# Attention with experts on one core: how the rough scores that set the softmax shift are made

## The chip, the cores and the metric

The kernel runs on one core of a Trainium2 chip. The metric is the device time of one execution in microseconds (us), lower is better. All times below are us unless marked ns.

## The reference, cut to what matters

Input x is 8 sequences of 512 tokens by 128 values, layer-normed. Then attention with 32 query heads and 16 key/value heads of width 64, a linear position bias and a causal mask; beside it a mixture of 8 experts, of which 2 serve each token; the two results are multiplied.

```python
scores = jnp.einsum('bhqd,bhkd->bhqk', q, k) / math.sqrt(HEAD_DIM)
scores = scores + bias[None]
scores = jnp.where(causal[None, None], scores, -jnp.inf)
attn = jax.nn.softmax(scores, axis=-1)
out = jnp.einsum('bhqk,bhkd->bhqd', attn, v)
...
s = _L0_attn_ref(xn, L0_attn_W_qkv, L0_attn_W_out)
g = _silu(_L0_ffn_ref(xn, ...))
x = x + s * g
```

## The kernel before, in words

The attention is cut into 64 bodies: one body is one sequence and one pair of key/value heads. A body has two slots (`sl`, one key/value head each), and a slot has two query heads (`h`), so a body makes four 512x512 causal score matrices. Bodies 0 to 31 run first, then the experts' blocks, at whose end the preparation of body 32 is mixed in, then bodies 32 to 63.

Numbers are held as two fp16 halves (hi and lo). A query head is stacked by DMA into `q_st` as 128 rows (64 of hi, 64 of lo) beside a second plane, whose rows 0 to 63 are hi again and whose row 64 holds one shift per query, in the row for the position bias; keys are stacked in `k_st` (two buffers, `par`, by the parity of the body). The softmax needs a shift per query near the row maximum. It is found from rough scores:

- M, `rough` (PE, L948 to L966): hi half of the queries times hi half of the keys, 64 rows each, the two heads of a slot as two products on the two halves of TensorE's rows, into the two banks `M_ps[0]` and `M_ps[1]`. Three rounds per slot (`ROUNDS`): query tiles 3; 0 and 2; 1. Six rounds in a body, 16 products of 128, 256, 384 or 512 columns.
- B, `peaks` (DVE, L1588): mask and minimum along each row of each of these products, one column of `spread` each; 12 tasks in a body.
- C, `turn_shifts` (PE, L968 to L977): four products of 128x128 with the identity turn `spread`, so that each head's shifts stand in one row (0, 32, 64, 96). `shifts` (ACT, L1284) copies each of the four rows, 1x512, into row 64 of the second plane of `q_st`.
- S (PE) makes the true scores of the causal part, transposed: ten groups in a body, alternating between two banks `S_ps`. E (ACT, L1295) takes the exponential of a group, L (POOL, L824) its low half, P (PE, L1025 to L1029) multiplies it with the values: 120 products in a body.
- N, A (DVE, ACT, SP) normalise and turn the result, O (PE) projects it. Q, K, V (PE) make the queries of a slot, the keys and the values; ACT then takes the hi half, DVE the lo half, SP issues the stacking DMAs (four for one slot's queries, two for one slot's keys).

What each engine does, and in which order, is a written list, `ORDER`, one table for each half: `("M0", 2, 87)` says that in window w the engine does task M0 of body w + 2; only the sequence counts, the third number merely places it. Each engine goes through its list strictly in order and waits on semaphores in front of each task, so a task that waits holds up all behind it on its engine. `G_USERS` says which of Q, K, V, O and C take turns in the two remaining PSUM banks. Before the change C of body w + 1 stands near the end of window w, and both slots' copies on ACT behind it; S0 of the next window waits for the first slot's copies (`crow0`). There is one buffer `q_st` per slot and head, so SP may stack the queries of body n only when the scores of body n - 1 are done; `q_hi` on ACT waits until the rough products have read `q_raw`.

Of the kernel before, what the change touches and what calls it, by code (L numbers as in the profile page):

```python
# [8 lines left out]
F16 = mybir.dt.float16  # L9
# [24 lines left out]
ROUNDS = [[(3, 0)], [(0, 0), (2, 128)], [(1, 0)]]  # L34
# [24 lines left out]
        [("V0", 1), ("Q0", 2), ("C0", 1)],  # L59
# [3 lines left out]
        [("V0", 1), ("Q0", 2), ("C0", 1)],  # L63
# [14 lines left out]
        ],  # L78
        "ACT": [
# [3 lines left out]
        ],  # L83
        "DVE": [
# [22 lines left out]
        ],  # L107
        "ACT": [
# [3 lines left out]
        ],  # L112
        "DVE": [
# [25 lines left out]
def build(nc, x, w_qkv, w_out, gate_w, gate_b, w1, b1, w2, b2, out):  # L139
    slopes = [float(s) for s in alibi_slopes()]  # L140
    ctx = ExitStack()
    with ctx:
# [1597 lines left out]
```

## Time and profile before

| | |
|---|---|
| median of 3 runs | 1191.23 (1187.22 to 1195.37) |
| profiled execution, its own time | 1190.88 |
| its span | 1189.1 |
| busy PE, DVE, ACT, POOL | 94%, 83%, 78%, 75% |
| rough products, L965, busy | 138.1 |
| `peaks`, L1588, busy | 451.7 |
| row copies, L1284, busy | 147.2 |

PE is TensorE's products, PEld its weight loads (they run beside products), DVE VectorE, ACT ScalarE, POOL GpSimd, SP the engine that issues most DMAs. A line such as `128*128 128x512` names a product with a 128-row, 128-column stationary operand and 512 moving columns. Successive products overlap, so the time a product holds TensorE is read from the starts of successive rows, not from its duration.

### The profile page before, as it was taken

The page shows a single profiled execution, that of the slowest core. Times are in us where ns is not written, and L with a number is a line of the kernel's source. Part 1 is how long each engine was busy: PE and PEld are TensorE (multiplying, and loading weights), DVE is VectorE, ACT ScalarE, POOL GpSimd, SP SyncE. Part 2 cuts the span into 40 slices and gives each one's busy share as a digit, 9 for nine tenths or more (in the row PEclk, how much of TensorE's full clock was granted, in tenths as well). Part 3 has the DMA queues.
Part 4 walks back from the last instruction along what each step waited for, and adds up shares of the span by engine and source line. Part 5 has one row for each costly group of instructions (what it writes and reads, how often), then busy time and mean ns, then how long its engine had stood idle before and what let it go on. Part 6 is the DMA issues. An engine that isn't in the chain of part 4 may idle for free.

```text
span 1189.1 us, 48527 instructions
## 1 busy us (share of the span) xinstructions
PE 1119.4 (94%) x16970; PEld 830.8 (70%) x16970; DVE 982.1 (83%) x3099; ACT 931.9 (78%) x1835; POOL 886.9 (75%) x1067
## 2 busy tenths in 40 slices
PE   2669999999999999998999989999999999999996
PEld 1447777777777777777888757777777777777775
DVE  7778888888888888886777878888888888888883
ACT  3548888888888888886666578888888888888884
POOL 7058998898988888885000068898989888899896
PEclk9579999999999999999999999999999999999998
DMA  8426765656656677656344437586765655655773
GB/s 246 182 54 114 132 137 132 136 132 134 137 127 136 132 133 135 132 132 97 77 91 112 83 85 131 130 134 132 127 133 133 132 120 130 140 130 130 134 131 80
DMA packets 268295, 150.34 MB, mean 126 GB/s; under 512 B 173360, under 2 KB 256672, under 8 KB 267424
## 3 DMA queue, kind: packets, MB, share of 16 engines
q1 hardware_dynamic: 263696, 138.72, 56.2%
q0 software_dynamic: 4096, 8.40, 3.0%
q8 instruction: 147, 2.41, 0.9%
q14 instruction: 84, 0.69, 0.2%
q10 hardware_dynamic: 272, 0.13, 0.0%
HBM read 15.76 MB, written 16.78 MB: 27 GB/s over the span
## 4 chain that ended last, share of the span: by engine, by line
PE 81%; POOL 4%; DVE 4%; issue 3%; DMA 2%; ACT 1%; SPq 0%; ACTq 0%; DVEq 0%; POOLq 0%
PE ps L993 12%; PE ps L899 8%; PE ps L965 8%; PE ps L900 7%; PE ps L901 7%; PE outs L1025 7%; PE ps L997 6%; PE outs L1029 6%; PE outs L1027 6%; PE ps L994 4%; POOL t_lo L824 3%; PE ps L1002 2%; PE ps L976 1%; PE outs L900 1%; PE outs L899 1%
## 5 line engine op out<-in xcount | busy, mean ns | idle before, releaser
L824 POOL TENSOR_TENSOR t_lo<-stage 128x512 f16<-128x512 f32 x640 | 652.7, 1038 | 103.9 <-ACT stage L1295 100.6
L1588 DVE CUSTOM_DVE_ANT_0 stage<-ps,kmask 128x512 bf16<-128x512 f32 (+3 forms) x1024 | 451.7, 488 | 108.6 <-PE ps L965 97.0
L1295 ACT ACTIVATE stage<-ps,slope 128x512 f32<-128x512 f32 (+1 forms) x768 | 440.3, 618 | 80.9 <-PE ps L1002 74.2
L993 PE MATMUL ps<-q_st,k_st 128*128 128x256 f16 (+3 forms) x1024 | 299.7, 302 | 2.8 <-ACT stage L1295 1.6
L1025 PE MATMUL outs<-v_sp,stage 128*128 128x65 f16 x2560 | 263.6, 195 | 3.4 <-POOL t_lo L824 2.9
L1027 PE MATMUL outs<-v_sp,stage 128*128 128x64 f16 x2560 | 262.6, 194 | 0.0
L1029 PE MATMUL outs<-v_sp,t_lo 128*128 128x65 f16 x2560 | 262.4, 194 | 0.0
L1025 PEld LDWEIGHTS outs<-v_sp,stage 128*128 128x128 bf16 x2560 | 235.1, 98 | 26.1 <-issue 14.3
L1027 PEld LDWEIGHTS outs<-v_sp,stage 128*128 128x128 bf16 x2560 | 235.6, 99 | 0.0
L1029 PEld LDWEIGHTS outs<-v_sp,t_lo 128*128 128x128 f16 x2560 | 235.2, 98 | 0.0
L994 PE MATMUL ps<-q_st,k_st 128*128 128x128 f16 x1024 | 223.5, 218 | 0.0
L997 PE MATMUL ps<-q_st,k_st 67*128 67x384 f16 (+2 forms) x768 | 210.6, 274 | 0.0
L1284 ACT CAST q_st<-ps 1x512 f16<-1x512 f32 x256 | 147.2, 575 | 49.0 <-PE ps L976 45.7
L965 PE MATMUL ps<-k_st,stage 64*128 64x512 f16 (+3 forms) x1024 | 138.1, 307 | 14.7 <-DVE spread L1588 10.5
L993 PEld LDWEIGHTS ps<-q_st,k_st 128*128 128x128 f16 x1024 | 100.0, 98 | 58.1 <-issue 33.4
L1002 PE MATMUL ps<-late_q,late_k 66*128 66x134 f16 (+1 forms) x640 | 135.6, 212 | 0.0
L779 POOL COPY slot_now<-slot_of 128x2 uint32<-128x2 uint32 x64 | 11.8, 184 | 138.7 <-DMA slot_y<-stage 138.7
L1236 ACT ACTIVATE stage<-ps,qscale 128x512 f16<-128x512 f32 x128 | 88.1, 688 | 30.2 <-PE ps L901 24.3
L997 PEld LDWEIGHTS ps<-q_st,k_st 67*128 67x128 f16 x768 | 74.4, 97 | 51.1 <-issue 0.9
L965 PEld LDWEIGHTS ps<-k_st,stage 64*128 64x128 f16 x1024 | 40.1, 94 | 97.4 <-issue 82.8
L994 PEld LDWEIGHTS ps<-q_st,k_st 128*128 128x128 f16 x1024 | 100.7, 98 | 10.6 <-issue 0.3
L1379 ACT ACTIVATE X<-ps,b1T 128x256 f32<-128x256 f32 x160 | 67.0, 470 | 47.1 <-PE ps L901 47.0
(220 smaller groups left out, 2694.1 us busy)
## 6 DMA issues: line engine op xcount, KB each, us to landing
q_st<-stage SPq DMA_DIRECT2D x256, 128.0 KB, 2.4
k_st<-stage SPq DMA_DIRECT2D x128, 128.0 KB
q_st<-stage SPq DMA_DIRECT2D x256, 64.0 KB, 2.1
k_st<-stage SPq DMA_DIRECT2D x128, 64.0 KB
slot_y<-stage SPq DMA_DIRECT2D x40, 128.0 KB, 2.0
slot_x<-att SPq DMA_DIRECT2D x2, 2048.0 KB, 8.9
wx_raw<-in_L_ffn_w SPq DMA_DIRECT2D x64, 64.0 KB
X<-in_L_attn_inputs SPq DMA_DIRECT2D x4, 512.0 KB, 9.9
```

The source lines that it names most:

```text
L824: pool.tensor_tensor(t_lo[r], t_p[r], upper(t_p[r]), ALU.subtract).then_inc(s[f"lo{u % NG}"], 1)
L965: mm = pe.matmul(M_ps[h][:, c0:c0 + w], q_raw[sl][head, 0, i * P:(i + 1) * P], k_st[par][sl][head, 0, 0:w], start=True, stop=True)
L993: pe.matmul(d, k[:, 0, at], q[:, 0, seen], start=(c0 == 0), stop=False, skip_group_check=True)
L994: pe.matmul(d[:, 0:P], k[:, 1, at], q[:, 1, at], start=False, stop=True, skip_group_check=True)
L997: pe.matmul(d[:, P:], k[far, 1, at], q[far, 1, (kt + 1) * P:SEQ], start=False, stop=True, skip_group_check=True)
L1002: pe.matmul(d, late_k[late, :], late_q[late, LATE:P].unsqueeze(1).to_broadcast([P - LATE - 1, len(first), P - LATE]), start=False, stop=Tr ...
L1025: pe.matmul(d, p_hi, v[:, with_one], start=(opens and i == kt), stop=False, skip_group_check=True)
L1027: pe.matmul(d[:, OUT_COL[sl]:OUT_COL[sl] + DH], p_hi, v[:, lo], start=False, stop=False, skip_group_check=True)
L1029: mm = pe.matmul(d, t_lo[r][:, c], v[:, with_one], start=False, stop=(closes and i == QT - 1), skip_group_check=True)
L1284: ins = act.copy(q_st[sl][h][DH:DH + 1, 1, :], bank_of("C0")[SHIFT[sl][h]:SHIFT[sl][h] + 1, :])
L1295: e = act.activation(t_p[r][:, c0:c1], S_ps[u % 2][:, c0:c1], ACT.Exp, scale=slope[:, bass.ds(pair_index(n) * 2 * SLOTS + sl * 2 + h, 1)])
L1588: ins = dve.tensor_tensor_reduce(junk[h][:, c0:c0 + w], M_ps[h][:, c0:c0 + w], kmask[:, SEQ - w:SEQ], -1.0 / 1024, 3e38, ALU.add, ALU.min, ...
```

## The change

The rough products take their queries from the stacked `q_st` (hi and lo, 128 rows) and their keys from the 128 stacked rows of `k_st`. They are one stream for both heads: five rounds per slot, each in one bank, the banks alternate, ten rounds in a body. The products themselves have the same numbers of columns as before. `q_st` becomes one tile per slot with both heads, in two buffers by the body's parity; SP stacks the queries of body n when the scores of body n - 2 are done. `spread` shrinks to 8 columns per slot, so C becomes one product per slot with an 8-column stationary operand; ACT copies its 8x128 result to `turned`, and a new SP task `set_shifts` sends that to the 1024 elements of row 64 by one DMA, for which the scores now wait (`row0`, `row1`). ACT's hi half of the queries no longer waits for the rough products. `ORDER` is rewritten for every engine; below stand PE, ACT and SP of the first half, the second half's table is rewritten likewise. In the start-up, steps of the routing hang on other tasks than before, and `pick` in the experts' part is an 8-column tile read with a repeated column.

```diff
-ROUNDS = [[(3, 0)], [(0, 0), (2, 128)], [(1, 0)]]
+
+ROUNDS = [[(0, 3, 0)], [(0, 0, 0), (0, 2, 128)], [(0, 1, 0), (1, 1, 256)], [(1, 3, 0)], [(1, 0, 0), (1, 2, 128)]]
...
         "PE": [
-            ("S0", 0, 0), ("M1", 1, 3), ("P9", -1, 5), ("S1", 0, 7), ("S2", 0, 11), ("Q1", 1, 14), ("M2", 1, 19),
-            ("V0", 1, 20), ("S3", 0, 25), ("S4", 0, 28), ("M3", 1, 32), ("K0", 2, 34), ("S5", 0, 38), ("P0", 0, 41),
-            ("P1", 0, 44), ("P2", 0, 47), ("M4", 1, 49), ("S6", 0, 51), ("S7", 0, 55), ("P3", 0, 58), ("P4", 0, 61),
-            ("Q0", 2, 63), ("M5", 1, 68), ("S8", 0, 69), ("S9", 0, 72), ("O0", -2, 76), ("C0", 1, 85),
-            ("M0", 2, 87), ("P5", 0, 89), ("P6", 0, 92), ("P7", 0, 94), ("P8", 0, 97),
+            ("S0", 0, 0), ("M8", 0, 1), ("M9", 0, 2), ("Q1", 1, 23), ("S1", 0, 25), ("P5", -1, 26), ("P6", -1, 27),
+            ("P7", -1, 29), ("P8", -1, 30), ("C1", 0, 37), ("P9", -1, 38), ("S2", 0, 38), ("M0", 1, 41), ("M1", 1, 49),
+            ("V0", 1, 55), ("S3", 0, 57), ("M2", 1, 60), ("K0", 2, 63), ("S4", 0, 63), ("M3", 1, 63), ("P0", 0, 64),
+            ("P1", 0, 64), ("M4", 1, 65), ("S5", 0, 65), ("P2", 0, 67), ("S6", 0, 67), ("P3", 0, 69), ("M5", 1, 70),
+            ("C0", 1, 75), ("M6", 1, 77), ("S7", 0, 78), ("Q0", 2, 79), ("P4", 0, 89), ("M7", 1, 91), ("S8", 0, 91),
+            ("O0", -2, 91), ("S9", 0, 96),
         ],
...
         "ACT": [
-            ("E0", 0, 5), ("E1", 0, 13), ("E2", 0, 17), ("Q1", 1, 22), ("A1", -1, 26), ("E3", 0, 30), ("E4", 0, 34),
-            ("V0", 1, 38), ("K0", 2, 41), ("R0", 2, 45), ("E5", 0, 47), ("W0", 1, 51), ("E6", 0, 57), ("E7", 0, 61),
-            ("Q0", 2, 70), ("A0", 0, 74), ("E8", 0, 77), ("E9", 0, 81), ("C0", 1, 89), ("C1", 1, 98),
+            ("E0", 0, 4), ("C1", 0, 6), ("E1", 0, 14), ("A1", -1, 14), ("E2", 0, 15), ("E3", 0, 25), ("V0", 1, 40),
+            ("E4", 0, 43), ("R0", 2, 48), ("K0", 2, 52), ("E5", 0, 60), ("E6", 0, 68), ("C0", 1, 71), ("E7", 0, 72),
+            ("Q0", 2, 75), ("E8", 0, 75), ("A0", 0, 77), ("E9", 0, 87), ("W0", 1, 88), ("Q1", 2, 90),
         ],
...
         "SP": [
-            ("W0", 1, 4), ("A0", -1, 13), ("Q0", 1, 33), ("K0", 2, 55), ("A1", -1, 64), ("Q1", 1, 78),
-            ("K1", 2, 96),
+            ("Q1", 1, 3), ("A0", -1, 8), ("A1", -1, 20), ("W0", 1, 54), ("C0", 1, 71), ("K0", 2, 73), ("Q0", 2, 81),
+            ("K1", 2, 91), ("C1", 1, 94),
         ],
...
-        q_st = [[sb(f"q_st{s}{h}", [P, 2, SEQ], F16) for h in range(2)] for s in range(SLOTS)]
+        q_st = [[sb(f"q_st{par}{s}", [P, 2, 2, SEQ], F16) for s in range(SLOTS)] for par in range(UNROLL)]
...
-        spread = [sb(f"spread{par}", [P, QT, P], F16) for par in range(UNROLL)]
+        spread = [sb(f"spread{par}", [P, SLOTS, 2 * QT], F16) for par in range(UNROLL)]
+        turned = [[sb(f"turned{par}{s}", [2 * QT, P], F16) for s in range(SLOTS)] for par in range(UNROLL)]
...
-        FILL_AT = {"M0": 84, "B0": 85, "B1": 85, "M1": 95, "M2": 18, "B4": 18, "B5": 18, "M3": 35, "B6": 35, "B7": 35, "M4": 51,
-                   "B8": 51, "B9": 51, "M5": 68, "B10": 68, "B11": 68}
+        FILL_AT = {"C0": 70}
...
+            def stack_queries(n, par, sl):
 
                 sp.wait_ge(s[f"ql{sl}"], n + 1)
                 sp.nop(nofuse=True)
-                slot_scored(sp, n - 1, sl)
+                slot_scored(sp, n - UNROLL, sl)
                 sp.nop(nofuse=True)
                 for h in range(2):
                     hi, lo = (q_raw[sl][DH * h:DH * h + DH, part, :] for part in range(2))
-                    sp.dma_start(q_st[sl][h][0:DH, :, :], hi.unsqueeze(1).to_broadcast([DH, 2, SEQ]))\
+                    to = q_st[par][sl][:, :, h, :]
+                    sp.dma_start(to[0:DH, :, :], hi.unsqueeze(1).to_broadcast([DH, 2, SEQ]))\
                       .then_inc(s[f"qst{sl}"], 16)
-                    sp.dma_start(q_st[sl][h][DH:2 * DH, 0, :], lo).then_inc(s[f"qst{sl}"], 16)
+                    sp.dma_start(to[DH:2 * DH, 0, :], lo).then_inc(s[f"qst{sl}"], 16)
+
+            def set_shifts(n, par, sl):
+
+                sp.wait_ge(s[f"crow{sl}"], n + 1)
+                sp.nop(nofuse=True)
+                if isinstance(n, int) and n == 0 and sl == 0:
+                    sp.wait_ge(s["copied"], 16 * len(COPIES))
+                    sp.nop(nofuse=True)
+                sp.dma_start(q_st[par][sl][DH:DH + 1, 1, :, :].rearrange("a h c -> a (h c)"), turned[par][sl][:, :])\
+                  .then_inc(s[f"row{sl}"], 16)
...
             def rough(n, par, j):
 
                 sl, r = divmod(j, NR)
-                need(pe, f"qh{sl}", n + 1)
+                need(pe, f"qst{sl}", (n + 1) * 64)
                 need(pe, f"kst{sl}", (n + 1) * 32)
-                for h in range(2):
-                    if r > 0:
-                        need(pe, f"peak{sl}{h}", n * NR + r)
-                    else:
-                        need(pe, f"peak{1 - sl}{h}", (n + sl) * NR)
                 if isinstance(n, int) and n == 0 and j == 0:
                     pe.wait_ge(s["xlo"], NB)
-
-                for i, c0 in ROUNDS[r]:
+                need(pe, "peak", n * NR * SLOTS + j - 1)
+                for h, i, c0 in ROUNDS[r]:
                     w = (i + 1) * P
-                    for h in range(2):
-                        head = slice(DH * h, DH * h + DH)
-                        mm = pe.matmul(M_ps[h][:, c0:c0 + w], q_raw[sl][head, 0, i * P:(i + 1) * P],
-                                       k_st[par][sl][head, 0, 0:w], start=True, stop=True)
-                mm.then_inc(s[f"rough{sl}"], 1)
-
-            def turn_shifts(n, par, _):
-
-                bank_free(n, "C0")
-                for sl in range(SLOTS):
-                    for h in range(2):
-                        need(pe, f"peak{sl}{h}", (n + 1) * NR)
-                for i in range(QT):
-                    mm = pe.matmul(bank_of("C0")[:, i * P:(i + 1) * P], spread[par][:, i, :], ident16[:, :],
-                                   start=True, stop=True)
-                mm.then_inc(s["turnc"], 1)
+                    mm = pe.matmul(M_ps[j % 2][:, c0:c0 + w], q_st[par][sl][:, 0, h, i * P:(i + 1) * P],
+                                   k_st[par][sl][:, 0, 0:w], start=True, stop=True)
+                mm.then_inc(s["rough"], 1)
+
+            def turn_shifts(n, par, sl):
+
+                bank_free(n, f"C{sl}")
+                need(pe, "peak", (n * SLOTS + sl + 1) * NR)
+                pe.matmul(bank_of(f"C{sl}")[0:2 * QT, 0:P], spread[par][:, sl, :], ident16[:, :], start=True, stop=True)\
+                  .then_inc(s[f"turnc{sl}"], 1)
 
             def scores(n, par, u):
 
                 sl = u // NG
                 need(pe, f"qst{sl}", (n + 1) * 64)
                 need(pe, f"kst{sl}", (n + 1) * 32)
-                need(pe, f"crow{sl}", n + 1)
+                need(pe, f"row{sl}", (n + 1) * 16)
...
-                need(act, f"rough{sl}", n * NR)
...
-            def shifts(n, _, sl):
-
-                act.wait_ge(s["turnc"], n + 1)
-                group_done(act, "scored", n - 1, sl * NG + NG - 1)
-                for h in range(2):
-                    ins = act.copy(q_st[sl][h][DH:DH + 1, 1, :], bank_of("C0")[SHIFT[sl][h]:SHIFT[sl][h] + 1, :])
-                ins.then_inc(s[f"crow{sl}"], 1)
+            def shifts(n, par, sl):
+
+                act.wait_ge(s[f"turnc{sl}"], n + 1)
+                need(act, f"row{sl}", (n + 1 - UNROLL) * 16)
+                act.copy(turned[par][sl][:, :], bank_of(f"C{sl}")[0:2 * QT, 0:P]).then_inc(s[f"crow{sl}"], 1)
...
             def peaks(n, par, j):
 
-                sl, r, h = round_of(j)
-                dve.wait_ge(s[f"rough{sl}"], n * NR + r + 1)
+                sl, r = divmod(j, NR)
+                dve.wait_ge(s["rough"], n * NR * SLOTS + j + 1)
                 dve.nop(nofuse=True)
-                if j < 2:
-                    need(dve, "turnc", n - UNROLL + 1)
+                if r == 0:
+                    need(dve, f"turnc{sl}", n - UNROLL + 1)
                     dve.nop(nofuse=True)
-                for i, c0 in ROUNDS[r]:
+                for h, i, c0 in ROUNDS[r]:
                     w = (i + 1) * P
                     ins = dve.tensor_tensor_reduce(
-                        junk[h][:, c0:c0 + w], M_ps[h][:, c0:c0 + w], kmask[:, SEQ - w:SEQ], -1.0 / 1024, 3e38,
-                        ALU.add, ALU.min, spread[par][:, i, SHIFT[sl][h]:SHIFT[sl][h] + 1])
-                ins.then_inc(s[f"peak{sl}{h}"], 1)
+                        junk[j % 2][:, c0:c0 + w], M_ps[j % 2][:, c0:c0 + w], kmask[:, SEQ - w:SEQ], -1.0 / 1024, 3e38,
+                        ALU.add, ALU.min, spread[par][:, sl, h * QT + i:h * QT + i + 1])
+                ins.then_inc(s["peak"], 1)
```

## Rows read from the trace of the kernel before

**Rows 1.** Page, the chain that ended last: shares of the span by engine.
```profile
PE 81%; POOL 4%; DVE 4%; issue 3%; DMA 2%; ACT 1%; SPq 0%; ACTq 0%; DVEq 0%; POOLq 0%
```

**Rows 2.** Windows: stretch, length, busy PE PEld DVE ACT POOL, clock, DMA, GB/s.
```profile
120.00:500.00 380.00, 378.76 (x5978) 276.52 (x5975) 329.08 (x1077) 322.53 (x629) 338.20 (x388) 1.00 0.65 133
560.00:690.00 130.00, 123.65 (x1524) 104.08 (x1522) 99.42 (x200) 80.98 (x202) 0.00 (x0) 1.00 0.44 91
720.00:1140.00 420.00, 416.70 (x6562) 305.47 (x6559) 362.25 (x1182) 357.54 (x687) 374.07 (x424) 1.00 0.65 131
1140.00:1189.10 49.10, 38.84 (x667) 30.67 (x664) 28.24 (x81) 30.97 (x60) 36.45 (x41) 0.92 0.47 98
```

**Rows 3.** Waits of PE, 120 to 500 us: total, times, longest.
```profile
PE outs L1025 <- POOL t_lo L824: 0.7, 3, 0.3
PE ps L965 <- issue: 0.4, 1, 0.4
```

**Rows 4.** Instructions of line 976 (turn), 300 to 450 us.
```profile
L976 PE MATMUL ps<-ident,spread x40: 218/219/220, 312.6 to 449.9; 128*128 128x128 f16 x40
```

**Rows 5.** Timeline of PE around two rough rounds: start, duration, instruction.
```profile
299.97 0.19 PE L1002 MATMUL ps<-late_q,late_k 66*128 66x67 f16 x1
300.10 0.39 PE L965 MATMUL ps<-k_st,stage 64*128 64x128 f16 x4
300.42 0.20 PE L1025 MATMUL outs<-v_sp,stage 128*128 128x65 f16 x1
...
302.25 0.38 PE L901 MATMUL ps<-xT_hi,wq_lo 128*128 128x512 f16 x1
302.56 0.28 PE L965 MATMUL ps<-k_st,stage 64*128 64x256 f16 x2
302.77 0.23 PE L899 MATMUL ps<-wv_hi,xT_hi 128*128 128x128 f16 x1
```

**Rows 6.** Timeline of PE, turn and the third kind of round.
```profile
312.53 0.22 PE L901 MATMUL ps<-wo_hi,aT 128*128 128x128 f16 x1
312.59 0.39 PE L976 MATMUL ps<-ident,spread 128*128 128x128 f16 x4
312.91 0.39 PE L965 MATMUL ps<-k_st,stage 64*128 64x512 f16 x2
313.23 0.20 PE L1025 MATMUL outs<-v_sp,stage 128*128 128x65 f16 x1
```

**Rows 7.** Timeline of PE, scores between 301 and 304 us.
```profile
301.30 0.27 PE L993 MATMUL ps<-q_st,k_st 128*128 128x256 f16 x1
301.41 0.22 PE L994 MATMUL ps<-q_st,k_st 128*128 128x128 f16 x1
...
303.45 0.38 PE L993 MATMUL ps<-q_st,k_st 128*128 128x512 f16 x1
303.67 0.22 PE L994 MATMUL ps<-q_st,k_st 128*128 128x128 f16 x1
303.73 0.33 PE L997 MATMUL ps<-q_st,k_st 67*128 67x384 f16 x1
303.89 0.19 PE L1002 MATMUL ps<-late_q,late_k 66*128 66x67 f16 x1
```

**Rows 8.** Page, costliest groups: busy, mean ns of one, idle before, releaser.
```profile
L824 POOL TENSOR_TENSOR t_lo<-stage 128x512 f16<-128x512 f32 x640 | 652.7, 1038 | 103.9 <-ACT stage L1295 100.6
L1588 DVE CUSTOM_DVE_ANT_0 stage<-ps,kmask 128x512 bf16<-128x512 f32 (+3 forms) x1024 | 451.7, 488 | 108.6 <-PE ps L965 97.0
L1284 ACT CAST q_st<-ps 1x512 f16<-1x512 f32 x256 | 147.2, 575 | 49.0 <-PE ps L976 45.7
```

**Rows 9.** Page, DMA issues: count, KB each, us from issue to landing.
```profile
q_st<-stage SPq DMA_DIRECT2D x256, 128.0 KB, 2.4
```

**Rows 10.** Timeline of SP: what one issue takes.
```profile
299.97 0.61 SPq L560 DMA_DIRECT2D q_st<-stage  x1
```

**Rows 11.** Timeline of ACT in front of the last body.
```profile
1148.41 2.35 ACT L1284 CAST q_st<-ps 1x512 f16<-1x512 f32 x4 [0.96 <-PE ps L976]
```

More of the change, by code:

```diff
@@ L58 @@
         [("Q1", 1), ("K0", 2), ("O0", -2)],
-        [("V0", 1), ("Q0", 2), ("C0", 1)],
+        [("C1", 0), ("V0", 1), ("C0", 1), ("Q0", 2)],
     ],
@@ L62 @@
         [("Q1", 1), ("K0", 2), ("O0", -2)],
-        [("V0", 1), ("Q0", 2), ("C0", 1)],
+        [("C1", 0), ("V0", 1), ("C0", 1), ("Q0", 2)],
     ],
@@ L281, in build @@
             tangent sigmoid summed gated partial fresh rd0 rd1 nrm0 nrm1 op acc ta0 ta1 ah0 ah1 al0 al1 rows
-            turnc crow0 crow1 copied
+            rough peak turnc0 turnc1 crow0 crow1 row0 row1 copied
             qst0 qst1 kst0 kst1 scales
@@ L291, in build @@
                 s[f"{step}{u}"] = sem(f"s_{step}{u}")
-        for sl in range(SLOTS):
-            s[f"rough{sl}"] = sem(f"s_rough{sl}")
-            for h in range(2):
-                s[f"peak{sl}{h}"] = sem(f"s_peak{sl}{h}")
         block = ctx.enter_context(nc.Block())
@@ L516, in batch_index @@
             return n // PAIRS
-        COPIES = [(k_st[0][1], k_st[0][0]), (k_st[1][0], k_st[0][0]), (k_st[1][1], k_st[0][0]),
-                  (q_st[1][0], q_st[0][0]), (q_st[1][1], q_st[0][1])]
-        ROW_STEPS = 3 + 2 + 5 + 2 * 4
+        k_const, q_const = k_st[0][0][DH:P, 1, :], q_st[0][0][DH:P, 1, 0, :]
+        COPIES = [(k_st[par][sl][DH:P, 1, :], k_const) for par, sl in ((0, 1), (1, 0), (1, 1))]\
+            + [(q_st[0][0][DH:P, 1, 1, :], q_const)]\
+            + [(q_st[par][sl][DH:P, 1, :, :], q_const.unsqueeze(1).to_broadcast([P - DH, 2, SEQ]))
+               for par, sl in ((0, 1), (1, 0), (1, 1))]
+        ROW_STEPS = 3 + 2 + 5 + 4
         ot = out.rearrange("b (t p) d -> p (b t) d", p=P)
@@ L591, in load_weights @@
                     sp.dma_start(wx_raw[:, k, :], w).then_inc(s["w_in"], 16)
-            stacks = {"Q": stack_queries, "K": stack_keys, "A": turn_out}
+            stacks = {"Q": stack_queries, "K": stack_keys, "A": turn_out, "C": set_shifts}
             go_ahead("SP", stacks, 0, HALF)
@@ L705, in _ @@
             mark(late_q[:, :], LATE)
-            k, q = k_st[0][0][:, 1, :], (q_st[0][0][:, 1, :], q_st[0][1][:, 1, :])
+            k, q = k_st[0][0][:, 1, :], q_st[0][0][:, 1, 0, :]
             row(pool.memset(k[DH:P, :], HIDE_K))
@@ L712, in _ @@
             row(pool.memset(k[DH:DH + 1, :], 1024.0))
-            for h in range(2):
-                row(pool.memset(q[h][DH:P, :], 0.0))
-                mark(q[h][DH:P, :], DH - MARKS)
-                row(pool.iota(q[h][DH:MARKS, :], [[P, QT], [0, P]], base=0, channel_multiplier=0,
-                              allow_small_or_imprecise_dtypes=True))
-                row(pool.memset(q[h][DH:DH + 2, :], 1.0))
+            row(pool.memset(q[DH:P, :], 0.0))
+            mark(q[DH:P, :], DH - MARKS)
+            row(pool.iota(q[DH:MARKS, :], [[P, QT], [0, P]], base=0, channel_multiplier=0,
+                          allow_small_or_imprecise_dtypes=True))
+            row(pool.memset(q[DH:DH + 2, :], 1.0))
             pool.iota(eidx[:, :], [[1, E]], base=0, channel_multiplier=0,
@@ L755, in pick_step @@
                 pool.wait_ge(s["small"], picked_steps)
-            pick_step(pool.memset(pick[:, :, :], 0.0))
+            pick_step(pool.memset(pick[:, :], 0.0))
             for row in (0, 32):
-                pick_step(pool.affine_select(out=pick[:, :, :], in_=pick[:, :, :], compare_op=ALU.not_equal, fill=1.0,
-                                             base=-row, pattern=[[-1, E], [0, P]], channel_multiplier=1))
+                pick_step(pool.affine_select(out=pick[:, :], in_=pick[:, :], compare_op=ALU.not_equal, fill=1.0,
+                                             base=-row, pattern=[[-1, E]], channel_multiplier=1))
             pool.wait_ge(s["sm"], 80)
@@ L991, in scores @@
                     at, seen = slice(kt * P, (kt + 1) * P), slice(kt * P, SEQ)
-                    k, q = k_st[par][sl], q_st[sl][h]
+                    k, q = k_st[par][sl], q_st[par][sl][:, :, h, :]
                     pe.matmul(d, k[:, 0, at], q[:, 0, seen], start=(c0 == 0), stop=False, skip_group_check=True)
@@ L1190, in _ @@
                         step_of(i_, c, g)
-            for sl in range(SLOTS):
-                for h in range(2):
-                    pe.wait_ge(s[f"peak{sl}{h}"], HALF * NR)
+            pe.wait_ge(s["peak"], HALF * NR * SLOTS)
             for sl in range(SLOTS):
@@ L1357, in _ @@
             act.wait_ge(s["consts"], 9)
-            run_bodies("ACT", {**tasks, "W": weights_hi, "R": send_hi}, 0, HALF)
+            run_bodies("ACT", {**tasks, "W": weights_hi, "R": send_hi, "Y": keep_ranks}, 0, HALF)
             leave_bodies("ACT", {**tasks, "W": weights_hi, "R": send_hi}, 0, HALF)
@@ L1667, in _ @@
             dve.wait_ge(s["attz"], 1)
-            enter_bodies("DVE", {**tasks, "Y": choose}, 0, HALF)
+            enter_bodies("DVE", {**tasks, "Y": choose_or_route}, 0, HALF)
             dve.wait_ge(s["zeros"], 16 * ZERO_DMAS)
-            run_bodies("DVE", {**tasks, "Y": lambda k: route(k - CHOICES)}, 0, HALF)
-            leave_bodies("DVE", {**tasks, "Y": lambda k: route(k - CHOICES)}, 0, HALF, late=LATE_O)
+            run_bodies("DVE", {**tasks, "Y": choose_or_route}, 0, HALF)
+            leave_bodies("DVE", {**tasks, "Y": choose_or_route}, 0, HALF, late=LATE_O)
             def parts(j, c, g):
```

38 lines of the change are left out of this document (16 added, 22 removed), and 34 rows, old and new, of the table ORDER.

## The prediction

> **What bounds the kernel now.** I read the chain of waits first: TensorE (PE) holds 81% of the span, no other engine more than 4% [rows 1]. The windows say where: in both attention stretches PE is busy for 378.8 of 380 and 416.7 of 420 us at full clock, DVE about 87%, POOL 89%, ACT 85%; even in the experts' part PE is busy 95% [rows 2]. The list of PE's waits for 120 to 500 us adds up to 1.1 us [rows 3]. So a body lasts as long as PE's own instruction stream. The turn (line 976) gives the period: 40 products are ten bodies; from the first start to the last, less three products of the same turn, (449.9 - 312.6 - 0.17) / 9 = 15.24 us [rows 4]. What counts is what each edit does to that stream; and, since a busy PE isn't a PE at its peak, I take the price of a product from the distance between starts, not from its duration.
>
> **Prices of a full-height product.** 512 columns hold PE for 303.67 - 303.45 = 0.22, 384 columns 0.16, 256 columns 0.11 [rows 7]; 128 columns half of the last, 0.055 (the starts, 0.06 apart, agree [rows 6, 7]). That is the column count at 2.4 GHz. Row counts of 67 or 66 instead of 128 change nothing (the 0.16 is a 67-row product).
>
> **What the rough rounds cost now.** They are the only 64-row products. The two heads do run together. Yet from line 1002 to the next values' product there are 0.45, less 0.03 for its own 67 columns is 0.42, where 128 and 384 columns streamed once are 0.215. The 256-column pair: 0.52 less 0.22 of line 901 is 0.30, against 0.11 streamed [rows 5]. The 512-column pair: the four turn products hold 4 x 0.055 = 0.22 of the 0.32 up to its start, which leaves 0.10 in front of it; from its start to the next product are 0.32, 0.10 over its 0.22 [rows 6]. So each round pays 0.10 going in and 0.10 coming out. Per slot 0.42 + 0.30 + 0.42 = 1.14, per body 2.28, of which 1.2 are these passages and not columns.
>
> Here the Trainium skill bears on the rows. Its page TensorEngine Tiling (Array Packing), Theoretical Speedup, gives products with at most 64 rows up to twice the rate when tiled; by that alone, giving up the pairs would add the 1.09 per body that streaming once takes, about 68 us in all, 1259. The same page, Key Properties, says that changing the tiling mode drains the engine. The rows show both, and the passages eat what the pairing saves, so the first rule alone is no case of its own here.
>
> **What they cost after.** One stream of 128-row products: (0.22 + 0.16 + 0.11 + 0.055) for each of four heads = 2.18 per body, without passages, since they stand among products of the same height. Change: -0.10 per body. Ten waits in place of six cost nothing when already met: score and value groups begin with such waits too, and are followed at column rate [rows 7].
>
> **The turn.** Before, four products of 0.055, 0.22. After, two of 128 moving columns, 0.11: -0.11 per body. But their stationary operand is 8 columns wide, and no product in the trace is narrower than 128 columns. This is the unknown cost. Lower bound nothing: the 67-row products show that a shape short of full need not cost. Upper bound the passage of the 64-row product: 2 turns x (0.10 + 0.10) = 0.40 per body. 8 of 128 lies on the side of 64 rather than of 67, a half or less of the array, so I take the upper end, slightly reduced, because the 0.10 going in covers a load of 128 columns and here 8 are loaded: 2 x (0.075 + 0.10) = 0.35. A gain below nothing I exclude: the 128 moving columns must stream.
>
> By the same page of the Trainium skill, Tiling Modes and Key Properties, a 128x32 tile is another mode, and entering it drains. No run here shows that for columns.
>
> **Sum on PE.** -0.10 - 0.11 + 0.35 = +0.14 per body; with the full 0.40 it is +0.19, with nothing -0.21. Bodies in which PE sets the time: 64 less the first two, 62 (the first stand before 120 us, in the start-up; body 32's preparation runs in the experts' part, also PE's). 62 x 0.14 = +8.7 us.
>
> **Off PE.** ACT loses four copies of 575 ns [rows 8], 2.3 per body, and gains two copies of 8x128, at most 575 each. ACT isn't late now, PE doesn't wait for it [rows 3], so this is worth nothing in the steady stretches. It is worth something where four copies stand on the path: in front of the last body 2.35 [rows 11]. Of that I take 1.5, because POOL's ten tasks of 1.04 [rows 8] soon set the pace there and keep some. Start-up: the rough products of body 0 now wait for stacking, which is issued long before; its six selection steps on DVE stay in one window. Nothing taken. DVE makes the same 16 reductions; a product and its reduction are now apart by one bank instead of two heads. POOL is not touched.
>
> **New waits.** The shifts go ACT, SP, DMA before the scores: at most 0.58 for the copy, 0.61 for the issue [rows 10], 2.4 to land [rows 9], 3.6 in all. On PE between C1 and S5 (first half) stand three score groups of 0.47 (512, 128 and 384 columns and the late product [rows 7]), five rounds of 0.22, V0 (12 x 0.055 = 0.66), K0 (3 x 0.22 = 0.66): 3.8, and three value groups of 12 products of 65 columns, 0.027 each at 2.4 GHz, 1.0. Slack 1.2. Covered. Tighter: SP's list has C1 of this body directly ahead of the stacking of slot 1's queries for the next, so if ACT's copy is late, four issues, then A0, A1 and the weights' DMAs wait. From C1: 0.58 + 0.61 + four issues of 0.61 + 2.4 = 6.0 till M5 may start; PE has between C1 and M5 five score groups 2.35, five rounds 1.1, V0 and K0 1.3, five value groups 1.6: 6.4. Slack 0.4 with the dearest copy, more with a shorter one. SP itself has room: two issues more, 1.2 in 15.2. The second `q_st` buffer takes away SP's wait for the previous scores, which none of PE's waits goes back to today: nothing.
>
> **Forecast.** Against the profiled execution, 1190.88 (span 1189.1; the median is 1191.23, 0.3 apart, so nothing to correct): 1190.9 + 8.7 - 1.5 = 1198, 0.6% slower. With the full passage price 1190.9 + 11.8 - 1.5 = 1201; its own range is 1192 to 1204. One per cent is about what a measurement of this kernel can tell from no change.
>
> **Rivals.** (B) The narrow turn pays no passage. Then 62 x -0.21 = -13.0, and 1190.9 - 13.0 - 1.5 = 1176. For it: the 66- and 67-row products flow at column rate; against it: the only products of half height or less in the trace pay. The page's drain rule, if it didn't hold for columns, is this case. (C) The slower side: SP's queue. If C1's copy reaches ACT behind an exponential (E0 stands before it, E1 behind it), set_shifts holds the stacking of the queries, M5 waits, and with it all of PE's list; and E1 behind a late C1 delays S3. It decides from a slack of 0.4 on: each 0.3 beyond is 62 x 0.3 = 18.6, so 1198 + 19 = 1217. For it: the computed slack is the smallest in the order, and both ACT and SP are strict lists. Against it: the copy of 8x128 is probably far below 575, and ACT now has 2 us less to do. (D) That the change doesn't do what it says, as 128-row products not reaching the column rate: the score products on the same tiles do, so I give it nothing.
>
> **How the numbers follow.** Forecast 0.52, B 0.25, C 0.23. Range: the forecast's 1192 to 1204 widened down to B with its scatter, 1173, and up over the near part of C, 1213. Faster by over 1% (below 1179): most of B, 0.19. Within 1%: the rest of B 0.06, the forecast but for 0.10, 0.42, and a mild C 0.03, together 0.51. Slower by over 1% (above 1203): 0.10 + 0.20 = 0.30.
>
> **What would show it.** In the timeline of PE, rough products of 512 columns spaced 0.22 and nothing in front or behind; the two turn products each with some 0.17 beyond their 0.055 (B: none). The period of the body 15.4 (B 15.0, C 15.7 or more). In the waits of PE, C would show the rough products or the scores waiting for a DMA into `q_st`, or for ACT's exponential. The last body's first exponential should come without four copies ahead. I am wrong if PE's waits grow beyond a few us, or if the period moves by something that isn't in the rough products or the turn.

## The result: 1.6% slower, and the profile after

The changed kernel takes 1210.64 us (median of 4, 1205.69 to 1212.28) against 1191.62 for the kernel before in the same runs: ratio 1.016 [1.0134, 1.019]. A second series, on another chip, gave 1205.37 against 1187.89, 1.015 [1.0133, 1.0169]. The profiled span is 1209.2, 20.1 more than before.

The page of the changed kernel: busy time by engine, and the chain that ended last by engine.

```profile
PE 1134.2 (94%) x16842; PEld 889.7 (74%) x16842; DVE 978.6 (81%) x3099; ACT 833.3 (69%) x1707; POOL 880.9 (73%) x1063
...
PE 68%; SPq 11%; DVE 6%; POOL 5%; DMA 5%; issue 4%; ACT 2%; ACTq 0%; DVEq 0%; POOLq 0%
```

ACT is 99 us less busy, and yet the kernel is slower. What matters is that the chain, 81% PE before [rows 1], is now 68% PE, and that SP's queue and DMA, 2% before, are 16% of it.

The windows of the changed kernel, against [rows 2]:

```profile
120.00:500.00 380.00, 372.46 (x5753) 289.68 (x5750) 314.35 (x1045) 278.61 (x561) 328.60 (x375) 1.00 0.63 129
...
690.00:720.00 30.00, 21.46 (x229) 14.72 (x227) 16.99 (x54) 15.33 (x32) 11.53 (x13) 0.89 0.27 68
720.00:1140.00 420.00, 416.96 (x6477) 327.56 (x6474) 362.45 (x1178) 309.79 (x627) 372.21 (x419) 1.00 0.68 131
```

PE's idle time in the first attention stretch went from 1.2 to 7.5 us, and fewer products (5753, before 5978) stand in it; some 50 of the difference are turn products that no longer exist. The second stretch is as full as before. Where body 32 starts, 690 to 720, PE is busy 21.5 of 30. To place the 20 us, take the start of the first late product (line 1002, now 996) of some bodies:

| | body 2 | body 31 | body 32 | body 33 | body 63 | end of span |
|---|---|---|---|---|---|---|
| before | 102.7 | 541.6 | 691.0 | 707.5 | 1164.7 | 1189.1 |
| after | 96.4 | 549.2 | 699.4 | 721.8 | 1181.8 | 1209.2 |
| difference | -6.3 | +7.6 | +8.4 | +14.3 | +17.1 | +20.1 |

The step from one column to the next tells where the time went: start-up -6.3, first half +13.9, experts' part +0.8, body 32 alone +5.9, second half +2.8, end +3.0.

**PE's own stream.** The timeline of PE in the changed kernel, a turn in the second half, twice, and the rough product in front of one in the first half; last, two turns of the kernel before in the second half:

```profile
761.67 0.19 PE L1023 MATMUL outs<-v_sp,t_lo 128*128 128x65 f16 x1
761.80 0.22 PE L971 MATMUL ps<-ident,spread 128*8 128x128 f16 x1
761.95 0.39 PE L987 MATMUL ps<-q_st,k_st 128*128 128x512 f16 x1
...
776.99 0.22 PE L971 MATMUL ps<-ident,spread 128*8 128x128 f16 x1
...
465.98 0.38 PE L963 MATMUL ps<-k_st,q_st 128*128 128x512 f16 x1
466.29 0.22 PE L971 MATMUL ps<-ident,spread 128*8 128x128 f16 x1
```

```profile
749.72 0.40 PE L976 MATMUL ps<-ident,spread 128*128 128x128 f16 x4
...
764.81 0.40 PE L976 MATMUL ps<-ident,spread 128*128 128x128 f16 x4
```

From the last values' product to the turn are 0.13, of which 0.03 is that product: 0.10 going in. From the turn to the next product 0.15, less 0.055: 0.10 coming out. The 512-column rough product holds 0.31 - 0.10 = 0.21, column rate. And the period of a body in which PE waits for nothing is 776.99 - 761.80 = 15.19, where before it is 764.81 - 749.72 = 15.09 to 15.10. The wide stream and the narrow turn together cost +0.09 per body. Thirty times that is 2.7, near the +2.8 of the second half, but that the two are the same isn't shown: PE's waits differ too, and in another profiled execution of the changed kernel (`e9_after` below) this stretch took 457.5 where it took 460.0 here and 457.2 before.

**What the first half waits for.** Waits of PE in the changed kernel, 120 to 500 us, against [rows 3], and the turns there:

```profile
PE outs L1019 <- POOL t_lo L829: 3.7, 6, 0.7
PE ps L963 <- DMA q_st<-stage: 3.2, 6, 0.8
...
L971 PE MATMUL ps<-ident,spread x49: 219/219/220, 122.2 to 498.2; 128*8 128x128 f16 x49
```

49 turns are 24 bodies, (498.2 - 122.2) / 24 = 15.67 each. Before it was 15.24 between 300 and 450 us [rows 4] and 15.19 over the same stretch as here, so 0.43 to 0.48 more, of which PE's stream, 0.09, is about a fifth. The two waits are two different chains. One is POOL:

```profile
226.51 1.05 POOL L829 TENSOR_TENSOR t_lo<-stage 128x512 f16<-128x512 f32 x1
227.51 0.67 POOL L834 TENSOR_TENSOR wx_lo<-wx_raw,wx_hi 128x256 f16<-128x256 f32 x1
228.14 0.42 POOL L797 TENSOR_TENSOR row_now<-mix,row_now 128x128 f16<-128x128 f32 x1
...
228.65 2.03 POOL L829 TENSOR_TENSOR t_lo<-stage 128x512 f16<-128x512 f32 x2
...
229.73 0.20 PE L1019 MATMUL outs<-v_sp,stage 128*128 128x65 f16 x1 [0.68 <-POOL t_lo L829]
```

The rewritten list puts the weights' low half (W0, L834) and the send task (I0, L797) between the low halves L0 and L1; P1 on PE waits for L1. I0 stood there before too; W0 came to it. All six waits for POOL lie between 150 and 325 us.

The other is SP's queue. The six waits for `q_st` lie between 380 and 493 us, and each is the first rough product M0 waiting for slot 0's queries. This is SP over one body there (its list from one `set_shifts` to the same one of the next body), and the PE row M0, which waits for the queries issued from 470.52 on:

```profile
459.63 0.71 SPq L565 DMA_DIRECT2D q_st<-turned  x1
460.50 0.65 SPq L554 DMA_DIRECT2D q_st<-stage  x1
...
463.26 2.68 SPq L586 DMA_TRANSPOSE aT<-stage  x2
466.04 2.16 SPq L597 DMA_DIRECT2D wx_raw<-in_L_ffn_w  x2
468.31 0.72 SPq L565 DMA_DIRECT2D q_st<-turned  x1
...
470.52 0.64 SPq L554 DMA_DIRECT2D q_st<-stage  x1
...
473.26 1.65 SPq L576 DMA_DIRECT2D k_st<-stage  x1
...
475.66 0.70 SPq L565 DMA_DIRECT2D q_st<-turned  x1
...
476.34 0.61 PE L963 MATMUL ps<-k_st,q_st 128*128 128x512 f16 x3 [0.82 <-DMA q_st<-stage]
```

One issue follows the other with 0.04 to 0.2 between them, and SP waits for nobody: the chain that ended last runs through SP's queue alone from 428.2 to 488.6 us. One body's list takes 475.66 - 459.63 = 16.03 there (15.65 and 15.76 in the two bodies before), more than the 15.19 of PE's stream. So late in the first half it is SP that sets the time. SP's own waits, 120 to 500 us, first before, then after the change:

```profile
SPq L555 <- PE ps L1002: 44.2, 47, 1.8
```

```profile
SPq L561 <- ACT turned L1274: 18.5, 23, 1.4
SPq L548 <- DVE stage L1592: 7.6, 10, 1.1
```

With 5.3 more for DVE, SP waited 49.5 us in this stretch before, 26.1 after, and from 428 to 489 us it waits once, 1.4 at the start. Most of its waiting before was for the scores of the body before, because there was one buffer for the queries.

At the end of the second half it is a chain of waits instead. The chain that ended last in the changed kernel there (start, duration, what):

```profile
1153.46 0.71 DVE outs L1623
...
1154.19 0.59 ACT stage L1268
...
1154.81 0.62 DVE stage L1614
1155.43 0.73 DVE stage L1592
...
1158.30 3.72 DMA q_st<-stage
1162.07 0.39 PE ps L963
```

DVE normalises slot 1 (N1), waits for ACT's copy of that, takes its low half (A1), and only then the low half of the next queries (Q1); then come three of SP's four issues, the landing, and the rough product M5, the first of slot 1. M5 waits five times in the second half, 0.3 to 0.9 each, M0 twice; behind some of these waits stands this chain, behind others SP's queue. Before, the rough products took the queries from ACT's output and needed none of this.

### The profile page after: what moved, and what is told of

It is laid out like the page before. It is cut to its first block, busy times and chain, and to the rows that moved or that the text cites. A ratio compares the mean times of both kernels' runs of the same rounds, so it can differ in the third digit from the quotient of the medians.

```text
span 1209.2 us, 48137 instructions
## 1 busy us (share of the span) xinstructions
PE 1134.2 (94%) x16842; PEld 889.7 (74%) x16842; DVE 978.6 (81%) x3099; ACT 833.3 (69%) x1707; POOL 880.9 (73%) x1063
## 3 DMA queue, kind: packets, MB, share of 16 engines
HBM read 15.76 MB, written 16.78 MB: 27 GB/s over the span
## 4 chain that ended last, share of the span: by engine, by line
PE 68%; SPq 11%; DVE 6%; POOL 5%; DMA 5%; issue 4%; ACT 2%; ACTq 0%; DVEq 0%; POOLq 0%
PE ps L963 9%; PE ps L987 8%; PE ps L904 6%; PE ps L906 6%; PE ps L905 6%; PE outs L1019 5%; PE ps L991 5%; PE outs L1023 5%; PE outs L1021 5%; DMA q_st<-stage 3%; PE ps L988 3%; SPq L554 3%; POOL t_lo L829 3%; SPq L556 2%; PE ps L996 2%
## 5 line engine op out<-in xcount | busy, mean ns | idle before, releaser
L1284 ACT ACTIVATE stage<-ps,slope 128x512 f32<-128x512 f32 (+1 forms) x768 | 455.9, 615 | 176.4 <-PE ps L996 160.8
L1584 DVE CUSTOM_DVE_ANT_0 stage<-ps,kmask 128x256 bf16<-128x256 f32 (+3 forms) x1024 | 455.3, 487 | 75.5 <-PE ps L963 73.5
L1019 PE MATMUL outs<-v_sp,stage 128*128 128x65 f16 x2560 | 282.5, 195 | 18.9 <-POOL t_lo L829 12.2
L1023 PE MATMUL outs<-v_sp,t_lo 128*128 128x65 f16 x2560 | 281.6, 194 | 0.0
L1021 PE MATMUL outs<-v_sp,stage 128*128 128x64 f16 x2560 | 281.4, 194 | 0.0
L963 PE MATMUL ps<-k_st,q_st 128*128 128x256 f16 (+3 forms) x1024 | 226.8, 302 | 14.9 <-DMA q_st<-stage 7.3
L963 PEld LDWEIGHTS ps<-k_st,q_st 128*128 128x128 f16 x1024 | 79.1, 98 | 57.3 <-issue 13.5
L1268 ACT CAST stage<-outs 128x512 f16<-128x512 f32 x128 | 73.8, 577 | 57.0 <-DVE outs L1623 53.9
L784 POOL COPY slot_now<-slot_of 128x2 uint32<-128x2 uint32 x64 | 11.4, 178 | 138.2 <-DMA slot_y<-stage 138.2
L1614 DVE TENSOR_TENSOR stage<-outs,stage 128x512 f16<-128x512 f32 x128 | 87.8, 686 | 22.6 <-ACT stage L1268 22.5
```

Of the source, the lines that this page charges most:

```text
L963: mm = pe.matmul(M_ps[j % 2][:, c0:c0 + w], q_st[par][sl][:, 0, h, i * P:(i + 1) * P], k_st[par][sl][:, 0, 0:w], start=True, stop=True)
L1019: pe.matmul(d, p_hi, v[:, with_one], start=(opens and i == kt), stop=False, skip_group_check=True)
L1021: pe.matmul(d[:, OUT_COL[sl]:OUT_COL[sl] + DH], p_hi, v[:, lo], start=False, stop=False, skip_group_check=True)
L1023: mm = pe.matmul(d, t_lo[r][:, c], v[:, with_one], start=False, stop=(closes and i == QT - 1), skip_group_check=True)
L1284: e = act.activation(t_p[r][:, c0:c1], S_ps[u % 2][:, c0:c1], ACT.Exp, scale=slope[:, bass.ds(pair_index(n) * 2 * SLOTS + sl * 2 + h, 1)])
L1584: ins = dve.tensor_tensor_reduce(junk[j % 2][:, c0:c0 + w], M_ps[j % 2][:, c0:c0 + w], kmask[:, SEQ - w:SEQ], -1.0 / 1024, 3e38, ALU.add, ...
```

## The experiments

All are edits of the changed kernel. Three chips were used; the kernel before took 1188.8, 1197.4 and 1187.9 on them, and it is the ratio to it on the same chip that compares.

**The turn at 128 columns** (`e1_turn128`; the added columns are zeros)

```diff
-        spread = [sb(f"spread{par}", [P, SLOTS, 2 * QT], F16) for par in range(UNROLL)]
+        spread = [sb(f"spread{par}", [P, SLOTS, 128], F16) for par in range(UNROLL)]
...
-                pe.matmul(bank_of(f"C{sl}")[0:2 * QT, 0:P], spread[par][:, sl, :], ident16[:, :], start=True, stop=True)\
+                pe.matmul(bank_of(f"C{sl}")[0:128, 0:P], spread[par][:, sl, :], ident16[:, :], start=True, stop=True)\
```

> The turn's stationary operand padded to 128 columns (columns 8 to 127 are zeros), all else as after the change. Theory 1 (PE's stream sets the time; the narrow turn pays a passage going in and coming out): the gaps of about 0.09 us in front of and behind each turn vanish, four per body, so the floor of the body's period falls from 15.20 to 14.8 and the time from 1210.6 by about 62 x 0.38 = 24 to 1187. Theory 2 (a loop through DVE, SP and the landing of the stacked queries is about as long as PE's stream): the gaps vanish too, but PE waits for DMA into q_st and for POOL instead, and the time falls by less than 8, to 1203 or more. Theory 3 (8 columns cost nothing special): no change.

Measured: 1195.14, ratio 1.0057 [1.0043, 1.007], about 1.0% under the changed kernel's 1.015 to 1.016: 11 to 13 us. Timeline of PE, second half:

```profile
751.73 0.19 PE L1023 MATMUL outs<-v_sp,t_lo 128*128 128x65 f16 x1
751.76 0.22 PE L971 MATMUL ps<-ident,spread 128*128 128x128 f16 x1
751.81 0.38 PE L987 MATMUL ps<-q_st,k_st 128*128 128x512 f16 x1
...
766.64 0.22 PE L971 MATMUL ps<-ident,spread 128*128 128x128 f16 x1
```

The passages are gone (0.03 and 0.05), and the period of an undisturbed body there is 14.88 (in the first half 14.80). But only half of the 24 us came back. Its waits of PE for 120 to 500 us:

```profile
PE ps L963 <- DMA q_st<-stage: 5.6, 7, 1.3
```

5.6 for the stacked queries, 3.2 with the narrow turn; 4.0 for POOL, 3.7 before that. The result lies between theories 1 and 2, and both hold in part: in most bodies of the second half PE's stream sets the time, in most of the first half POOL or SP's queue, which gain little from a shorter stream. The profiled executions don't split the gain cleanly between the halves: from body 2 to 31 this kernel takes 447.8, the changed one 452.8 (449.7 in `e9_after`), from 33 to 63 it takes 454.2, the changed one 460.0 (457.5).

**72 and 64 columns** (`e2_turn72`, `e3_turn64`; the same two lines with 72 and 64)

> The same with 72 columns. If what matters is that more than half of the columns are used, as with the 66- and 67-row products, the gaps at the turn vanish as with 128 columns. If any operand narrower than 128 columns pays, they stay near 0.09 us each.

> The same with 64 columns. If half or less of the columns pays, the gaps at the turn are those of the 8-column turn, 0.09 to 0.10 us in front and behind; the weight load of 64 instead of 8 columns would show as a longer gap in front, by up to 0.03 us.

Timelines of PE, first 72, then 64 columns:

```profile
751.09 0.19 PE L1023 MATMUL outs<-v_sp,t_lo 128*128 128x65 f16 x1
751.12 0.23 PE L971 MATMUL ps<-ident,spread 128*72 128x128 f16 x1
751.18 0.38 PE L987 MATMUL ps<-q_st,k_st 128*128 128x512 f16 x1
```

```profile
759.89 0.19 PE L1023 MATMUL outs<-v_sp,t_lo 128*128 128x65 f16 x1
760.01 0.24 PE L971 MATMUL ps<-ident,spread 128*64 128x128 f16 x1
760.19 0.39 PE L987 MATMUL ps<-q_st,k_st 128*128 128x512 f16 x1
```

72 columns pay nothing (one run, 1195.17), 64 pay 0.09 in and 0.12 out (one run, 1208.06). So the edge lies between 64 and 72 columns, as that of the rows lies between 64 and 66. The 64-column operand doesn't lengthen the gap in front: the load isn't what is waited for, and my small rebate for the 8-column load was wrong.

**The last store ahead of the stacking** (`e4_store_first`)

```diff
                 for c in range(STEP):
                     loads_and_stores(j, c)
+                    if (j, c) == (STEPS - 1, STEP - 1):
+                        store(STEPS - 1, STEP - 1)
                     for g in range(PARTS):
                         begin_half("SP", stacks, HALF, BODIES, fill_part(j, c, g))
-            store(STEPS - 1, STEP - 1)
```

> At the end of the experts' part SP issues the last store to slot_y ahead of the stacking of body 33's queries and keys, not behind it. If the 6 us that body 32 lost are POOL's wait for that store (it stands in front of POOL's low halves, and PE waits 3.4 and 1.4 for these), the store goes out some 5 us earlier and the time falls by 4 to 6, to about 1205. If PE's own late rough rounds cause it, less than 2.

Measured: 1200.14, ratio 1.009 [1.0074, 1.0105], 0.6 to 0.7% under the changed kernel, 7 to 8 us, more than the 4 to 6 expected. In the changed kernel SP's timeline has

```profile
701.41 0.60 SPq L577 DMA_DIRECT2D k_st<-stage  x1
702.05 0.58 SPq L622 DMA_DIRECT2D slot_y<-stage  x1
```

and in PE's timeline the values of body 32 follow late:

```profile
707.41 0.24 PE L1019 MATMUL outs<-v_sp,stage 128*128 128x65 f16 x1 [3.35 <-POOL t_lo L829]
...
709.62 0.24 PE L1019 MATMUL outs<-v_sp,stage 128*128 128x65 f16 x1 [1.37 <-POOL t_lo L829]
```

With the store first POOL's wait for it is 134.7 instead of 138.2 us, and body 32 takes 18.5 instead of 22.4. Those 4 us are shown; where the rest of the gain comes from stays open.

**Order edits** (`e5_pool`, `e6_late_m`, both, with the first and fourth experiment, in `e7_all`, and DVE's order on top in `e8_all_q0`)

```diff
-            ("D1", 0, 8), ("L0", 0, 10), ("W0", 0, 12), ("I0", 1, 14), ("L1", 0, 16), ("L2", 0, 22), ("L3", 0, 25),
+            ("D1", 0, 8), ("L0", 0, 10), ("L1", 0, 16), ("L2", 0, 22), ("W0", 0, 23), ("L3", 0, 25), ("I0", 1, 26),
```

```diff
-            ("P7", -1, 29), ("P8", -1, 30), ("C1", 0, 37), ("P9", -1, 38), ("S2", 0, 38), ("M0", 1, 41), ("M1", 1, 49),
-            ("V0", 1, 55), ("S3", 0, 57), ...
+            ("P7", -1, 29), ("P8", -1, 30), ("C1", 0, 37), ("P9", -1, 38), ("S2", 0, 38),
+            ("V0", 1, 55), ("M0", 1, 55), ("M1", 1, 56), ("S3", 0, 57), ...
...
-            ... ("S3", 0, 15), ("M0", 1, 15), ("M1", 1, 15), ("V0", 1, 17), ...
+            ... ("S3", 0, 15), ("V0", 1, 15), ("M0", 1, 16), ("M1", 1, 17), ...
```

```diff
-            ("B6", 1, 71), ("N0", 0, 73), ("Q0", 2, 77), ("B7", 1, 78), ...
+            ("B6", 1, 71), ("Q0", 2, 72), ("N0", 0, 77), ("B7", 1, 78), ...
```

> First half only: on POOL the weights' task W0 and the send task I0 stand behind the low halves L2 and L3, not between L0 and L1. If the stalls of 0.84 us in front of the values' products of P1, five of them between 110 and 330 us, come from W0 and I0 in front of L1, they vanish and the time falls by 4 to 6 us from the changed kernel's. If POOL as a whole is late (its rate is the limit), they move to another group and the gain is under 2.

> Rough rounds M0 and M1 stand behind V0 on PE in both halves, 0.67 us later. If the waits for DMA into q_st (M0 waiting for the stacking of slot 0, 0.2 to 1.0 us each, nine from 380 us on) are a chain just too long, these lose up to 0.67 each and the time falls by 3 to 6 us. If the chain is a closed loop longer than the period, M0 later only moves its end, and the time stays within 2 us.

> Together: turn with 128 columns, last store first, W0 and I0 later on POOL, M0 and M1 behind V0. If PE's stream sets the time once these four are mended: the 1195.1 of the wide turn less 8 (store), less 5 (POOL), less 5 (M0): about 1177, 1% below the kernel before. If a loop through the queues takes over, above 1185.

> The same, and in the first half DVE takes the low half of slot 0's queries ahead of normalising slot 0, about 0.9 us earlier. If DVE's order is what makes the stacking late, another 2 to 5 us less than with the four; if the landing of the DMA or SP's issues are, within 1 us of it.

Measured, on the chip where before takes 1197.4: 1.0425, 1.0584, 1.0365, 1.0371. The first three are misses, and not by anything that I had expected. The fourth is within 1 us of the third (1242.9 against 1241.9), the case in which DVE's order isn't what makes the stacking late; but PE stood still elsewhere in these runs, so it tests little. Waits of PE in `e5_pool`, 120 to 500 us:

```profile
PE outs L1019 <- issue: 9.3, 24, 0.5
PE outs L1023 <- issue: 7.8, 20, 0.7
PE outs L1021 <- issue: 7.8, 20, 0.5
```

PE stands still, waiting for no semaphore that the profile shows, always late in the run P5 to P9 of short products around C1. Its list in this kernel is the changed kernel's own, only POOL's differs. The waits for POOL are gone from the list, as expected. From body 2 to 31 it takes 499.3 where the changed kernel took 452.8; from body 33 to 63, where PE's list has that run cut by score groups, 458.6 and 460.0. That called for the same kernels on another chip.

**The same again, and the run cut in two** (`e9_after` unedited, `e10_split`, `e11_two` with the wide turn and the store alone, `e12_all_again` the kernel of `e7_all`)

```diff
-            ("S0", 0, 0), ("M8", 0, 1), ("M9", 0, 2), ("Q1", 1, 23), ("S1", 0, 25), ("P5", -1, 26), ("P6", -1, 27),
+            ("S0", 0, 0), ("M8", 0, 1), ("M9", 0, 2), ("Q1", 1, 23), ("P5", -1, 23), ("P6", -1, 24), ("S1", 0, 25),
```

> The changed kernel once more, unedited, on the chip of the next three. The four order edits ran on another chip (before: 1197 there, 1189 on the chip of the first four) and lost 1.3 to 2 us per body of the first half in gaps in which PE waits for nothing visible, all late in the run of 48 to 60 short values' products P5 to P9 around the turn. Theory 1 (that chip supplies PE's instructions more slowly, and a long run of products 0.03 apart uses them faster than they come): unedited it is as slow there, about 1250, though PE's list is untouched. Theory 2 (the edits caused it): 1.6% above before on any chip.

> The four edits, and P5 and P6 ahead of S1, so that the run of short products is cut into 24 and 36 with a score group between them. Theory 1: on the slow chip the gaps fall by more than half, and the time with them, to 1205 or less; on the other chip no difference from the four edits. Theory 2: no difference on either chip.

> Wide turn and last store first, no edit of the order. The two gains add: on a chip where before takes 1189, 1195.1 less 8 is 1187, the same as before within 0.3%. On the slow chip the long run of short products is still there, and it is 1.03 or more times before.

> The four edits (wide turn, last store first, W0 and I0 later on POOL, M0 and M1 behind V0) once more. On the chip where before takes 1189, by theory 1 the order edits do what they were meant to and it takes about 1177, 0.99 of before; by theory 2 it is 1.036 times before on this chip too.

Measured, on the chip where before takes 1187.9: 1.0151 [1.0133, 1.0169], 1.0007 [0.9988, 1.0025], 0.9997 [0.9985, 1.0009], 1.0005 [0.9994, 1.0017]. The kernel of `e7_all` is thus 1.0365 on one chip and 1.0005 on another, and the standing still is not there on the latter: the edits alone don't cause it, that chip or its state is needed for it. Whether the changed kernel without edits would show it there isn't known; the kernel before doesn't, to judge by its 1197.4. That PE's instructions come too slowly there is argued from the place behind 40 products 0.03 apart, not shown; the packets of the instruction queue (q8 in the profile) took no longer, 1.14 us each in `e5_pool` and 1.15 in `e12_all_again` between 120 and 500 us. The slow chip wasn't met again, so neither the unedited kernel nor the cut run was timed on it, and `e10_split`, as fast as `e12_all_again` on a chip without the trouble, decides nothing.

`e11_two` did what was expected of it: 1.0% and 0.6% add up, and the changed kernel is as fast as the one before. The order edits on top gave nothing, where I had expected 10 us. The waits of PE in `e12_all_again`, 120 to 500 us, point to the reason:

```profile
PE ps L964 <- DVE spread L1585: 9.7, 24, 0.7
PE ps L964 <- DMA q_st<-stage: 1.9, 5, 0.6
```

POOL is gone from the list, so W0 and I0 were what L1 stood behind, and the wait for stacked queries fell from 5.6 in `e11_two` to 1.9. But M0 behind V0 now stands only one score group ahead of M2, which writes the same bank and must wait for DVE's reduction of M0, in every body: 24 waits in 24 bodies, and no body of the first half takes less than 15.33 now, where the shortest take 14.84 in `e11_two`. That longer body also gives SP more time for its list, so the 1.9 isn't all the edit's merit. No run shortened SP's list; that it would give back the rest of the first half is argued from the rows above.

## Why the prediction was right in range and wrong in its point

The time lies in the range, near its upper end; the likeliest case, 1198, within 1%, didn't come. 1217 for the slower side, at 0.30 for more than 1%, was nearer. That it is inside has some luck in it: the start-up gave back 6.3 that nobody had forecast, and without them it would be 1217, above the range's 1213. By the prediction's own signs it was (C)'s case more than the forecast's: the body of the first half takes 15.67, where (C) has 15.7, rough products waited for a DMA into `q_st`, and PE's idle time in the first stretch grew from 1.2 to 7.5.

- **Bound by PE's stream, and its prices.** Right. Starts give the price: rough products at column rate, 2.18 for 2.28, and no passages around them.
- **The narrow turn.** Right that it pays like a 64-row product: 0.10 + 0.10 per turn, 0.39 per body where I took 0.35; (B) is excluded. Net per body +0.09, forecast +0.14. With the measured 0.39 my own sum would be +0.18. The stream without passages is as forecast, 14.88 in the wide turn's second half against 15.10 before, -0.22 for -0.21; but there the narrow turn lengthens the body by 15.19 - 14.88 = 0.31 only, and in the first half, where it is 15.19 - 14.80 = 0.39, the stream without passages is 0.30 shorter than before. Where these 0.09 lie stays open. The Trainium skill's page TensorEngine Tiling (Array Packing), Key Properties, has the drain on a change of mode; 64 rows against 67 and 64 columns against 72 agree with it, 0.09 to 0.12 us each way against nothing. Priced alone, the turn costs 24 us of PE's stream, of which removing the passages returned 11 to 13.
- **"SP itself has room: two issues more, 1.2 in 15.2."** This is the step that failed. In the first half SP has 18 issues in a body, 16 before. The two new ones take 0.70 to 0.73 each and some 0.15 up to the next, 1.7 for the 1.2 that I took. Worse, I counted the new issues and not the whole list: with the short pauses between them a body's issues fill 14.4 us on average there (12.9 before), and late in the first half, where single issues of the keys and weights take 1.6 or more, 15.65 to 16.03 without a wait, where PE's stream has 15.19. Of the chain that ended last, 87 us between 120 and 500 us are SP's queue; before the change none.
- **New waits: "Covered", and the second buffer worth nothing.** I followed C1 to S5 and to M5 in the first half and found 1.2 and 0.4 of slack, which held: S5 doesn't show in PE's waits, M5 once, at 514 us. I did not follow slot 0: M0, which now needs its stack, came up to 0.8 late behind SP's full list. And I did not work out the second half, where M5 waits five times, behind DVE's N1, A1 and Q1 or SP's queue. (C) named SP's queue, strict lists and M5; it looked for the cause in ACT's late copy of C1, not in the length of SP's list, and it looked in the first half, where M0 waits.
- **"POOL is not touched."** Wrong. Its list was reordered like all others, and W0 and I0 in front of L1 stop PE for P1. After 29 bodies at 0.09, 11 of the first half's 13.9 us remain. The two chains' waits make 6.9 of them as the list above counts; a wait costs some 0.17 more than it says, because a product's start is followed by the next long before its printed end. The rest isn't traced.
- **Experts' part: no cost written.** Wrong by 5.9 at body 32: SP stacks body 33 ahead of the last store, for which POOL waits. Following SP's list to its end in that part would have found it. The store moved up returned 7 to 8 us, body 32 3.9 of them.
- **The end: -1.5.** Wrong sign, +3.0. The four copies are gone, but PE waits 2.1 for DVE's low half and 1.3 for POOL there. Before, it waited 0.3 for POOL and 0.8 for ACT. No run isolates this either.
- **Start-up: nothing.** It gave 6.3 back. The routing's steps on DVE stand behind more tasks than before (the one of line 1532 started at 63.3; as line 1521 it starts at 67.1); the first late product of body 1 starts at 69.7 instead of 87.5, that of body 2 at 96.4 instead of 102.7. No run isolates this.

## What to carry to other kernels

A lone product whose stationary operand has half or fewer of the rows or columns (64 rows, 64 or 8 columns here) is to be priced with two passages of 0.1 us, and can be padded: 120 zero columns were worth 1%. A queue to which issues are added has to be summed over its whole list for one body and set against the period, not only the new issues against the room that it seems to have. When an input of an early product changes from one engine's output to a tile stacked by DMA, follow it for every slot and in each half's list, not only for the edges that the diff adds. In a schedule written as lists for each engine, a task moved in any list is an edit: here one store behind four issues cost 7 to 8 us, the narrow turn 11 to 13.

## What the runs showed that I had not expected

- The passage has a sharp edge at half in both directions: 72 columns 0.03 and 0.06 around the turn, 64 columns 0.12 and 0.18; 67 rows nothing, 64 rows 0.10 each way.
- The same kernel can stand 1.0005 and 1.0365 to the same reference on two chips, with 28 us of PE standing still for nothing visible (9.3 + 7.8 + 7.8 + 3.4 between 120 and 500 us in `e5_pool`), in a long run of products 0.03 apart. For this kernel a ratio from one chip isn't enough.
- Between 120 and 500 us SP issues 436 DMAs, 400 before, and the queue that no row of engine busy time shows becomes the limit.
